# Scan units, group norm, transposes and output tiles in other places of a four-engine schedule

## The reference, cut to what matters

```python
# s: recurrent attention, x is the normed input, per head a 16x16 state
r, k, v, g = ((x + dx * lora(lerpx, z)) @ zW.T for z in "rkvg")
st = wt[..., None] * st + kv;  y = rt @ (st + u * kv)    # along the tokens
s = (silu(g) * layernorm(y over the 16 features of a head)) @ oW.T
# g: 16 heads of causal attention over a latent, then 8 experts (2 chosen) and a shared one
x = x + attention(rmsnorm(x));  g = x + moe(rmsnorm(x))
```

## Time and profile before

| | |
|---|---|
| timed runs | 2268.3, 2276.2, 2276.84 us |
| profiled execution | 2276.78 us, span 2275.0 us |
| TensorE's granted clock, mean over the span | 0.963 of full |
| busy PE, DVE | 2062.7 us (91%), 1794.2 us (79%) |
| busy ACT, POOL | 974.1 us (43%), 846.5 us (37%) |
| eighth start of L1927, and first | 2196.3 us, 721.1 us |

### The profile page before, as it was taken

The page is one execution under the profiler, slowest core; times in us unless marked ns, Lnnn a source line. Parts: engine busy times, 40 slices in busy tenths (PEclk is TensorE's granted clock), DMA queues, the critical chain, the costliest instruction groups (busy, mean ns, idle before and its releaser), DMA issues.

```text
span 2275.0 us, 37286 instructions
## 1 busy us (share of the span) xinstructions
PE 2062.7 (91%) x11722; PEld 1243.2 (55%) x11723; DVE 1794.2 (79%) x2906; ACT 974.1 (43%) x2556; POOL 846.5 (37%) x666
## 2 busy tenths in 40 slices
PE   7998599997988999998999889998989998899887
PEld 4554599997445445544554455455445544554554
DVE  5997466664697889779897988898798879887985
ACT  3444244442274237334623652373347235612741
POOL 1335200001543364336435542643364346326430
PEclk9999799998999999999999999999999999999998
DMA  6554411113222022211211230222122112302210
GB/s 174 145 158 138 146 54 54 52 55 116 64 57 80 1 65 71 61 37 47 66 47 47 61 86 4 61 66 70 29 56 66 47 47 57 79 15 60 61 48 10
DMA packets 145727, 151.18 MB, mean 66 GB/s; under 512 B 47664, under 2 KB 105648, under 8 KB 145584
## 3 DMA queue, kind: packets, MB, share of 16 engines
q1 hardware_dynamic: 138288, 136.73, 22.0%
q0 software_dynamic: 3072, 8.41, 1.1%
q10 hardware_dynamic: 4224, 4.19, 0.6%
HBM read 121.71 MB, written 27.43 MB: 66 GB/s over the span
## 4 chain that ended last, share of the span: by engine, by line
issue 24%; PE 23%; DVE 18%; POOL 8%; ACT 2%; DMA 0%; POOLq 0%; DVEq 0%; ACTq 0%
PE bank L1375 8%; PE bank L1238 4%; DVE arena L1777 4%; POOL arena L2064 3%; PE bank L1292 3%; DVE arena L1797 3%; DVE arena L1790 3%; PE bank L1255 3%; PE bank L1388 2%; POOL arena L2058 2%; DVE arena L2011 1%; ACT arena L1587 1%; POOL arena L2079 1%; PE bank L1265 1%; DVE arena L1852 1%
## 5 line engine op out<-in xcount | busy, mean ns | idle before, releaser
L2058 POOL TENSOR_TENSOR arena<-arena 128x512 f32<-128x512 f32 x256 | 337.1, 1319 | 567.9 <-DVE arena L1797 491.5
L1375 PE MATMUL bank<-arena 128*128 128x512 f32 (+2 forms) x1312 | 438.6, 489 | 6.8 <-DVE arena L1927 6.8
L1171 PE MATMUL bank<-arena 128*128 128x512 f32 (+2 forms) x768 | 360.5, 614 | 6.8 <-ACT arena L1542 5.4
L1797 DVE TENSOR_TENSOR_SCAN arena<-arena 128x512 f32<-128x512 f32 x256 | 361.9, 1414 | 1.7
L1587 ACT ACTIVATE arena<-bank,arena 128x128 f32<-128x128 f32 (+3 forms) x512 | 266.3, 531 | 194.9 <-DVE arena L1777 193.8
L1375 PEld LDWEIGHTS bank<-arena 128*128 128x128 f32 x1312 | 249.9, 203 | 177.2 <-issue 142.1
L1790 DVE TENSOR_TENSOR arena<-arena 128x512 f32<-128x512 f32 x256 | 249.0, 973 | 40.6 <-DMA arena<-values 36.5
L1238 PE MATMUL bank<-arena 64*128 64x128 f32 (+3 forms) x1024 | 207.5, 481 | 71.4 <-ACT arena L1587 49.7
L1171 PEld LDWEIGHTS bank<-arena 128*128 128x128 f32 (+2 forms) x768 | 139.5, 190 | 198.7 <-issue 171.5
L1777 DVE TENSOR_REDUCE arena<-bank 128x2 f32<-128x256 f32 (+3 forms) x256 | 206.9, 808 | 39.0 <-PE bank L1241 39.0
L1596 ACT ACTIVATE arena<-bank 128x128 f32<-128x128 f32 (+3 forms) x512 | 196.4, 441 | 72.3 <-PE bank L1255 72.3
(11 more groups left out here) (200 smaller groups left out, 2960.8 us busy)
## 6 DMA issues: line engine op xcount, KB each, us to landing
arena<-values SPq DMA_DIRECT2D x256, 256.0 KB, 3.4
arena<-in_L_attn_h SPq DMA_DIRECT2D x16, 512.0 KB, 10.4
arena<-in_W1T SPq DMA_DIRECT2D x8, 1024.0 KB
arena<-in_W2T SPq DMA_DIRECT2D x8, 1024.0 KB
sorted_rows<-arena SPq DMA_DIRECT2D x42, 128.5 KB, 9.9
arena<-sorted_rows SPq DMA_DIRECT2D x40, 128.5 KB, 2.1
arena<-in_b2row SPq DMA_DIRECT2D x40, 128.0 KB, 2.9
gate_rows<-arena SPq DMA_DIRECT2D x39, 128.0 KB, 1.7
```

The source lines that it names most:

```text
L1171: last = nc.tensor.matmul(dst[rows, :], w, x, start=(n == 0), stop=(n == len(pairs) - 1))
L1375: last = nc.tensor.matmul(dst[o], w, x, start=first, stop=last_one)
L1797: nc.vector.tensor_tensor_scan(state[n % STATES][:, 1:T + 1], proj["w"][:, m, :], kv[n % 2], VEC["init"][:, m * HD + j:m * HD + j + 1], AL ...
L2058: nc.gpsimd.tensor_tensor(prods[(n + 2) % PRODS], state[n % STATES][:, 0:T], proj["r"][:, m, :], ALU.mult).then_inc(prod_done, 1)
```

## The change

- `EARLY` 24 to 22, `STEPPED` 22 to 20, `AHEAD` 4 to 2. Units 2 and 3 leave `before_attention` for the loop, the loop still runs 18 units (2 to 19), and the experts get two more: units 25 to 31 now go behind experts 0 to 5. The products on GpSimd move alike.
- The reductions in the loop stand in steps 7, 14, 20 and 27 (before in 5, 11, 17 and 23, as `UNIT_STEP` gives). Group 4 goes from loop step 32 to behind `wo(1, early)` in the tail, group 5 from between the two halves of the `xc` transposes to expert 2, groups 6 and 7 from experts 2 and 6 to experts 4 and 8.
- In the loop `turn_probs` comes ahead of `weigh_values`, and at step 33 `wo(0, early)` ahead of `mean0`. `read_out(b, 0)` goes from step 25 to step 31.
- In the tail only `wo(1, early)` is ahead of the last parts of tiles 0 and 1; the first three groups of tiles 2 and 3 follow behind these.
- The second half's mean and variance leave the experts: `mean_last` stands behind the products `la_vk` and `la_rg`, `var_last` behind `lb_d`, and `center_last` and the square go to the start of `before_attention`. `ln_inv` and `ln_scale` follow the last blend. In the experts `read_out(b, 1)` and the first half's norm come one to three experts later. The last sequence does these steps at its end.
- `lat` goes from ahead of the queries to behind them; its copy on ScalarE stands in step 1 of the loop. The queries keep their banks.
- GpSimd's two `pow` steps of the head are parted: the first ahead of product 30, the second after the last product.

```diff
-EARLY = 24
-STEPPED = 22
-AHEAD = 4
+EARLY = 22
+STEPPED = 20
+AHEAD = 2
...
-QKV = "sp0 sp1 lat q2 q3 q4 q5 q6 q7".split()
+QKV = "sp0 sp1 q2 q3 q4 q5 q6 q7 lat".split()
...
-PRE_BANKS = ([6, 7, 3, 5, 0, 1, 2] + 5 * [3, 5, 6, 7, 0, 1, 2])[:len(PRE)]
+PRE_BANKS = ([6, 7, 3, 5, 0, 1, 2] + 5 * [3, 5, 6, 7, 0, 1, 2])[:len(PRE) - 7] + [0, 1, 2, 3, 5, 6, 7]
...
                 lora_a("vk", 0, 2)
                 lora_a("rg", 2, 2)
+                if ended is not None:
+                    mean_last(ended)
                 pe.wait_ge(a_read, pre.read(b, "la_vk"))
                 lora_pair(b, "v", "k", th[0])
                 lora_a("d", 4, 1)
                 pe.wait_ge(a_read, pre.read(b, "la_d"))
                 lora_b(b, "d", "d", th[2])
+                if ended is not None:
+                    var_last(ended)
...
                     if i == PSTEPS + 1:
+                        pe.wait_ge(y_out, GROUPS * b + GROUPS - 1)
+                        wo(0, early)
                         pe.wait_ge(y_read, 2 * b + 1)
                         result(b, "mean0", [(full, mean_m, y[:, 0, :], True, True)], bank[post.bank("mean0")])
-                        pe.wait_ge(y_out, GROUPS * b + GROUPS - 1)
-                        wo(0, early)
                         turn_probs(b, i - LAG)
-                    if i == PSTEPS:
-                        reduce_state(b, STEPPED // 4 - 1)
+                    if i < PSTEPS + 1:
+                        turn_probs(b, i - LAG)
                     done = i - LAG - 1
                     if done >= 0 and done % GSTEPS >= NT:
                         weigh_values(b, done // GSTEPS, done % NT)
-                    if i < PSTEPS + 1:
-                        turn_probs(b, i - LAG)
...
-                for i in range(1, NT):
-                    wo(i, early)
+                wo(1, early)
+                reduce_state(b, STEPPED // 4 - 1)
                 pe.wait_ge(y_out, GROUPS * b + GROUPS)
                 wo(0, [GROUPS - 1])
                 wo(1, [GROUPS - 1]).then_inc(made2, 2)
+                wo(2, early)
+                wo(3, early)
...
-                    if half:
-                        reduce_state(b, STEPPED // 4)
...
-                    if e == 2:
-                        reduce_state(b, EARLY // 4)
-                    elif e == 6:
-                        reduce_state(b, EARLY // 4 + 1)
-                    elif e == ME:
-                        mean_last(b)
+                    for at, g in ((2, 5), (4, 6), (ME, 7)):
+                        if e == at:
+                            reduce_state(b, g)
                     if e:
                         down(e - 1)
-                var_last(b)
...
-                for name in ("v0", "k0", "v1", "k1", "d0", "d1"):
+                if ended is not None:
+                    center_last(ended)
+                for name in ("v0", "k0", "v1", "k1", "d0", "d1", "r0", "g0", "r1", "g1"):
                     blend(name)
                 if ended is not None:
                     ln_inv(ended, 1)
                     ln_scale(ended, 1)
-                for name in ("r0", "g0", "r1", "g1"):
-                    blend(name)
-                if ended is not None:
                     ln_gate(ended, 1)
...
-                outer(b, 3)
                 if ended is not None:
                     gate_rows(ended, 1)
                     residual(ended)
-                scan(b, 2)
                 for name in QKV:
                     m = int(name[-1]) if name != "lat" else 0
-                    if name == "q2":
-                        unit(b, AHEAD - 1)
...
-                    if e < 4:
+                    if e < 6:
                         unit(b, EARLY + 4 + e)
-                    elif e == 5:
-                        read_out(b, 1)
+                    elif e == 6:
                         ln_inv(b, 0)
-                    elif e == 6:
+                    elif e == 7:
                         ln_scale(b, 0)
-                    elif e == 7:
-                        center_last(b)
                     elif e == 8:
                         ln_gate(b, 0)
+                        read_out(b, 1)
```

More of the change, by code:

```diff
@@ L1137, in sequence @@
                         store_sequence(b - 1)
-                    if n == EARLY + COPIES and not last:
+                    if n == 28 and not last:
                         sp.wait_ge(pv_mm, CHUNKS * b + 2 * CHUNKS)
@@ L1491, in _ @@
             experts(B - 1, True)
+            mean_last(B - 1)
+            var_last(B - 1)
             gates(B - 1, 0)
@@ L1576, in before_attention @@
                 nc.scalar.activation(x2, s_in, ACT.Copy).then_inc(x2_kept, 1)
-                act.wait_ge(made, pre.made(b, "lat"))
-                nc.scalar.activation(lat_tok.rearrange("p t c -> p (t c)"), bank[pre.bank("lat")][:, 0:NT * ND], ACT.Copy).then_inc(a_read, 1)
             def attention(b):
@@ L1620, in attention @@
                         exp(2 * i + 1)
+                    if i == LAG - 1:
+                        act.wait_ge(made, pre.made(b, "lat"))
+                        nc.scalar.activation(lat_tok.rearrange("p t c -> p (t c)"), bank[pre.bank("lat")][:, 0:NT * ND],
+                                             ACT.Copy).then_inc(a_read, 1)
                 act.wait_ge(pv_mm, CHUNKS * b + 2 * CHUNKS)
@@ L1891, in attention @@
                         highest(b, i)
+                    if i == PSTEPS - 1:
+                        read_out(b, 0)
                     if i >= GSTEPS + 1 and (i - GSTEPS - 1) % GSTEPS == 0:
@@ L1897, in attention @@
                         scale_values(b, (i - GSTEPS - 5) // GSTEPS)
-                    if i == UNIT_STEP[HD - 1] + 5:
-                        read_out(b, 0)
                 center()
@@ L2021, in _ @@
             experts(B - 1, True)
+            center_last(B - 1)
             ln_inv(B - 1, 1)
@@ L2042, in gather, with head_rstd, head_rms @@
                                          in_offset=bass.IndirectOffsetOnAxis(ap=idx[:, i:i + 1], axis=0)).then_inc(g_loaded, 16)
-            def head(b):
+            def head_rstd(b):
                 g.wait_ge(var_done, b + 1)
                 nc.gpsimd.tensor_tensor(rstd, var_eps, neg_half, ALU.pow).then_inc(rstd_done, 1)
+            def head_rms(b):
                 g.wait_ge(ms_done, b + 1)
@@ L2058, in product, with before_attention @@
                 nc.gpsimd.tensor_tensor(prods[(n + 2) % PRODS], state[n % STATES][:, 0:T], proj["r"][:, m, :], ALU.mult).then_inc(prod_done, 1)
-            def before_attention(b):
+            def before_attention(b, ended):
+                if ended is not None:
+                    square_last(ended)
                 for n, x in enumerate(MIX_ORDER):
@@ L2069, in before_attention @@
                         product(b, 1)
-                    elif n == 3:
-                        product(b, 2)
-                        product(b, 3)
                     name, rows = ("ckv", P) if n == 0 else (f"q{n - 1}", P)
@@ L2111, in experts, with square_last @@
                 for n in range(EARLY + 3, UNITS):
+                    if n == UNITS - 2 and not final:
+                        head_rstd(b + 1)
                     product(b, n)
                 if not final:
-                    head(b + 1)
+                    head_rms(b + 1)
+            def square_last(b):
                 g.wait_ge(last_read, 4 * b + 1 + 1)
@@ L2118, in _ @@
             gather(0)
-            head(0)
+            head_rstd(0)
+            head_rms(0)
             g.wait_ge(weights_in, 16 * NW)
-            before_attention(0)
+            before_attention(0, None)
             attention(0)
@@ L2124, in _ @@
                 experts(b, False)
-                before_attention(b + 1)
+                before_attention(b + 1, b)
                 attention(b + 1)
             experts(B - 1, True)
+            square_last(B - 1)
             g.wait_ge(g_loaded, 64 * B)
```

## The result

The changed kernel takes 2258.44 us (median of 5 runs, 2257.5 to 2260.01). The kernel before takes 2276.2 us (5 runs, 2268.3 to 2276.84). The ratio is 0.9934, with a 95% interval of 0.9919 to 0.995: a gain of 0.7%. The 23 later runs of the kernel before, made beside the experiments, have a median of 2270.33 (2267.97 to 2276.08); against them the gain is 12 us or 0.5%. The forecast was 2262. The profiled execution spans 2255.7 us at a mean granted clock of 0.957 (before 2275.0 and 0.963): the work is shorter and the clock is worse.

What follows compares the result with a forecast made beforehand. PE was taken as the bound on the whole, with PE and DVE near full and handing it over by stage. From 2276.78 us: -14 queries, -12 loop, 0 experts, 0 tail, +3 end, +8 clock give 2262; range 2243 to 2287.

Steps and rivals of the forecast that it cites:

- queries: Query rotations: DVE is relieved and q2 is ready earlier, 1.7 us gained a sequence, 2.5 in the first, together 14.
- loop: Attention loop: reductions moved to where DVE did not wait save 1.5 us a sequence, 12 us over eight loops.
- tail and experts: Two units fit into DVE's idle time in the experts, and the second `xc` half decides the tail: 0 each.
- end: Last sequence: mean to variance now form a chain, so the reciprocal begins later, +3 us, bounds 1 and 5.
- clock: Behind the tail: joined idle pieces make more tails take the long dip, +8 us, bounds 12 lost and 12 gained.
- the 1.5 that I credited to the reductions: Attention loop: 1.07 + 0.72 us of DVE's waits less 0.3 for the reductions' new places, 1.5 us a sequence.
- rival 2: Experts become bound by DVE and the change is slower: 3.4 us in each of 8 sequences, 2289 us; chance 0.15.
- two short tails: Two of the three tails with the short clock dip would take the long one, 4 us each, 8 us lost.
- Rival 1: Hand-over: another limit meets DVE's relief; loop 0, queries -7, end +3, clock +4, 2277 us; chance 0.27.
- Rival 3: Loop and clock: all DVE waits gained, 3.4 us eight times, and no clock loss, 2239 us; chance 0.11.
- The case of "slower": Whole kernel: a measured time over 2287.6 us, given a chance of 0.11.

Runs made afterwards that it cites:

- the filled kernel before: The kernel before plus matmuls nobody reads: one ahead of each half of `xc`, one ahead of the gate, two ahead of the variance; 2256.61 us.
- the kernel with the filled end: The changed kernel with unread matmuls in PE's gaps each sequence, plus nine more in the last sequence's end; 2220.46 us, ratio 0.9774.
- the filled pair: The kernel before and the changed kernel, both with unread matmuls in PE's idle gaps but none added at the end; 2256.61 and 2224.98 us.
- the units back: The changed kernel with scan units 2 and 3 back among the query rotations, three forms differing in the reductions' places; 2287.12, 2301.68 and 2282.58 us.
- the kernel of the group norm alone: The kernel before with only the second half's mean, centring, square and variance moved into `before_attention`; 2280.62 us, ratio 1.004.
- the kernel with the old order: The changed kernel with `weigh_values` ahead of `turn_probs` in the loop again; 2260.52 us, ratio 0.9955.
- the old tail: The changed kernel with tiles 1 to 3 early in one run and group 4's reduction back in loop step 32; 2283.52 us, ratio 1.0065.
- with `lat` ahead: The changed kernel with `lat` ahead of the queries again; 2260.02 us, ratio 0.9953.

## Why the prediction was right, and where it was not

The forecast was 3.6 us above the median, and the mechanism is the one it named: DVE was packed at the queries and interrupted in the loop, and both are relieved. Two errors in size partly cancelled, though: the gain was put 8 us too low, and 3 us of that were taken back by a clock term that was too small. That the total came so near is in part luck. The terms of the sum, against the stages at an even clock (the clock's term is what dips add, stage by stage, in the two kernels as they are):

| term | predicted | measured |
|---|---|---|
| start | 0 | -0.2 |
| queries | -14 | -18.3 |
| loop | -12 | -16.0 |
| tail and experts | 0 | +1.1 |
| end | +3 | +3.2 |
| clock | +8 | +10.9 |
| sum | -15 | -19.3 |

**Queries.** The rule "a product is ready then, so the rotation can start then" gave 1.7 us a sequence; seven sequences gave 2.0 to 2.1. The first one gave 4.0, where I had put 2.5: it takes 59.29 us in the filled kernel before and 55.15 in the kernel with the filled end, with dips of 11.2 and 11.0 us. (The 53.80 of the filled pair go with a dip of 8.2 us.) In single steps: mean and variance cost 1.5 us, the units' place gives 3.5, of which 1.2 hang on `lat` standing behind the queries. With the units back, `lat` behind them gives nothing (57.74 with it, 57.75 in the kernel of the group norm alone): it is PE's order that counts only once DVE is free to follow.

**Loop.** 2.0 to 2.1 us instead of 1.5, and two thirds of that are due to the order within a step that the prediction counted at nothing. This is the step that failed: it saw that ScalarE gets its input by a weighing earlier and counted nothing, since PE's time between two scores stays the same. In the example's loop ScalarE waits 8.7 us for the turned probabilities with the old order and 3.8 with the new one, and DVE's wait for scores is 4.3 and 2.4 us. PE's own wait for the exponential doesn't fall (5.6 and 6.6 us), so how the relief of ScalarE reaches the scores is argued and not shown. The other 0.7 (before to the kernel with the old order, 74.72 to 74.02) is what reductions, `read_out` and units bring together; the 1.5 that I credited to the reductions was too much. DVE's wait fell from 4.9 to 2.4 us, a little more than forecast.

**Experts.** Nothing, as predicted. DVE's longer list fits, and rival 2 is refuted. At an even clock the stage takes 56.7 us against 56.6. The nothing is a sum, as it was in the prediction: 0.9 us for two units and a reduction, and an estimated 1.6 us back for mean and variance. The 0.8 us that are missing between these and the +0.1 measured are not priced.

**Tail.** Its work is the same within 0.1 us, and the wait of 1.83 us became 3.27, as predicted (3).

**End.** The chain is there, and its place in the timeline is

```profile
2230.18 0.68 DVE L1808 TENSOR_TENSOR arena<-bank,arena 128x512 f32<-128x512 f32 x1
2230.92 1.13 PE L1303 MATMUL bank<-arena 128*128 128x512 f32 x2 [2.48 <-DVE arena L1808]
2232.09 0.69 DVE L1744 TENSOR_TENSOR arena<-arena,bank 128x512 f32<-128x512 f32 x1 [1.22 <-PE bank L1303]
2232.86 1.04 POOL L2116 TENSOR_TENSOR arena<-arena 128x512 f32<-128x512 f32 x1 [15.22 <-DVE arena L1744]
2233.95 2.08 PE L1307 MATMUL bank<-arena 128*128 128x512 f32 x2 [1.90 <-POOL arena L2116]
2236.78 3.35 DVE L1751 RECIPROCAL arena<-arena 128x512 f32<-128x512 f32 x1 [4.01 <-ACT arena L1550]
```

From read-out to reciprocal it takes 6.6 us, where I had summed 5: the variance alone runs for 2.08 us (1.13 in the earlier trace rows), since the clock fell while PE waited. The end cost 5.5 us instead of 3. The chain is not to blame: with fillers in both, the reciprocal starts 62.9 us behind the last `xc` against 59.7, which is 3.2 us and the forecast's 3. The other 2.3 us are the clock's. (The filled ends as wholes, 78.17 and 76.77 us, lie 1.4 us apart only because the first gate of the kernel before still takes 3.78 us at the low clock, where it takes 1.99 in the other.)

**Clock.** The sign was right, the size low and the place too narrow. I gave up two short tails at 4 us each. Of the long dip of 10.2 us the kernel before has five in eight tails; the kernel after has six, two of 6.8 us, and no short one. But a long dip costs 2.6 us in the experts (59.2 against 56.6) of the kernel before, not 4, and the 3.4 us dip there costs nothing (56.60 with it, 56.59 without). The 4 us came from 212.5 less 207.9, and 1.5 us of that are the dip in the long sequences' queries (57.8 against 56.28). By stages the 10.9 us are 1.8 in the experts and 1.8 in the tails, 2.4 in the queries (a dip in six of seven sequences, five before), 2.6 in the loop (two dips, none before) and 2.3 at the end. I had priced the dips in one stage only.

**Rivals.** Rival 1, the hand-over, was wrong in its size: the loop did shorten. Rival 3 was half right: more came, but not without the clock's loss. The case of "slower" exists in the kernels with the units back or the old tail, 2282.58 to 2301.68 us, and not in the change itself.

**Left open.** The 28 runs of the kernel before spread from 2268 to 2277 us, most of them at 2268 to 2271, and the profiled one lies at the upper end. Since the profile of a run at the lower end is lacking, I can't say which dips it is without. Against those runs the change is worth 10 to 13 us, against the upper ones 18. Nor is it shown what decides between a dip of 3.4, 6.8 and 10.2 us behind the same gap. The runs show that the dips of phase C follow idle pieces of PE and that fillers take dips away. An idle piece doesn't always bring one: the 1.9 us ahead of the variance stand in seven sequences of the kernel before, and a dip behind them in five.

## What to carry to other kernels

Where two engines hand the bound to each other, price a reordering by who waits for whom on every engine of the chain: a swap that costs the bound engine nothing can free a third one (1.3 us a loop here). Move a term out of a packed stretch before you reorder what feeds it, and don't price a part of a coupled change by undoing it alone. Compare two schedules once with their idle pieces filled: the clock hid some 11 of 30 us here, and filling the changed kernel's gaps brought 33 us more, about 3 of them in a stretch without fillers.

## What was not expected of the hardware

PE work that computes nothing makes the kernel faster: 2258.44 to 2224.98 us with six more products of 0.9 us each a sequence, in gaps of 0.8 to 3.3 us. The granted clock of the span goes from 0.957 to 0.980 by it. The Trainium skill, TensorE: Matmul & The Clock Gate, Part 1, has the gate follow how busy the engine has just been. The trace agrees: 0.957 without the fillers and 0.980 with them. One product of the three (0.9 us of 3.3 filled) takes no tail's dip away.

A dip comes back at places that the change did not touch: in the kernel of the group norm alone a new one stands at the first scores of seven sequences, and with `lat` ahead 207.1 and 209.3 us alternate from one sequence to the next. The clock couples stages that share no data, so that the totals of single edits don't add up: 2 us for the order of a step that is worth 8 x 1.3 us of loop, 24 us for the units, whose queries alone lose 30.7.
